# Attention kernel: softmax tiles as the stationary operand of the value products, and outputs reshaped through memory

## What is computed

```python
def _masked_attention(xf, Wq, Wk, Wv, lookahead):
    q = jnp.einsum('bnd,hed->bhne', xf, Wq)
    k = jnp.einsum('bnd,hed->bhne', xf, Wk)
    v = jnp.einsum('bnd,hed->bhne', xf, Wv)
    s = jnp.einsum('bhqe,bhke->bhqk', q, k) * scale
    mask = i[:, None] <= i[None, :] if lookahead else i[:, None] >= i[None, :]
    s = jnp.where(mask, s, jnp.finfo(s.dtype).min)
    p = jax.nn.softmax(s, axis=-1)
    return jnp.einsum('bhqk,bhke->bhqe', p, v)
...
o = jnp.concatenate([o_lb, o_la], axis=1)   # (B, 16, T*F, 64)
o = o.reshape(B, T * F, D)                  # no transpose: heads stay apart
out = jnp.einsum('bnd,od->bno', o, Wo)
return x + out
```

## Time and profile before

| | us |
|---|---|
| median of 3 runs | 3389.85 (3389.22 to 3391.37) |
| the profiled execution | 3386.05, span 3384.2 |
| TensorE busy | 3179.4 (94%), 14472 products |
| TensorE weight loads | 2443.1 (72%) |
| VectorE busy | 2062.4 (61%) |
| ScalarE busy | 1740.3 (51%) |
| GpSimd busy | 1672.8 (49%) |
| mean granted clock of TensorE | 0.986 |

### The profile page before, as it was taken

How to read it: one execution, slowest core, us unless ns; L and a number is a source line. 1 busy time by engine, 2 the same in 40 slices (tenths; PEclk the granted TensorE clock), 3 DMA queues, 4 the chain that set the end, 5 groups by cost and what they waited for, 6 DMA issues and landing times.

```text
span 3384.2 us, 50386 instructions
## 1 busy us (share of the span) xinstructions
PE 3179.4 (94%) x14472; PEld 2443.1 (72%) x14472; DVE 2062.4 (61%) x3452; ACT 1740.3 (51%) x3525; POOL 1672.8 (49%) x1306
## 2 busy tenths in 40 slices
PE   4999998999999679999999999999999999999998
PEld 3888887788888457766777767777777677767776
DVE  6212111410110488888888888888888887888885
ACT  2100110210100267777767777777777777777775
POOL 2000000100000367777777777777777777777774
PEclk9999999999999789999999999999999999999999
DMA  6325223422311232111212111212121112111210
GB/s 236 100 84 135 95 66 82 154 71 50 97 62 49 64 84 60 59 54 44 56 50 69 44 56 50 69 44 57 51 69 44 51 56 69 44 50 57 62 39 19
DMA packets 142547, 232.93 MB, mean 69 GB/s; under 512 B 76800, under 2 KB 76800, under 8 KB 142336
## 3 DMA queue, kind: packets, MB, share of 16 engines
q1 hardware_dynamic: 142336, 230.73, 22.9%
HBM read 163.58 MB, written 67.11 MB: 68 GB/s over the span
## 4 chain that ended last, share of the span: by engine, by line
PE 28%; POOL 13%; DVE 11%; issue 9%; DMA 1%; ACT 1%; POOLq 0%; DVEq 0%; SPq 0%; ACTq 0%
POOL p_low L691 6%; POOL k L716 4%; PE acc L1058 4%; PE acc L1062 4%; PE max L1014 4%; PE acc L1060 4%; PE scores L1044 4%; PE scores L1039 3%; DVE o_full L983 3%; PE rows L1076 3%; DVE part_max L929 2%; POOL q L712 2%; DVE p_low L691 2%; PE side L1024 1%; DVE diagonal L702 1%
## 5 line engine op out<-in xcount | busy, mean ns | idle before, releaser
L691 POOL TENSOR_TENSOR p_low<-probs,p_high 128x512 fp32r<-128x512 f32 (+2 forms) x960 | 1191.3, 1257 | 575.0 <-ACT p_high L864 539.3
L860 ACT ACTIVATE probs<-scores 128x512 f32<-128x512 f32 (+3 forms) x1280 | 684.1, 534 | 411.0 <-PE scores L1044 390.5
L929 DVE TENSOR_REDUCE part_max<-max 128x1 f32<-128x512 f32 (+3 forms) x1280 | 766.1, 603 | 197.8 <-PE max L1014 178.2
L864 ACT ACTIVATE p_high<-scores 128x512 fp32r<-128x512 f32 (+3 forms) x1280 | 683.3, 534 | 0.0
L1014 PE MATMUL max<-k,q 128*128 128x512 f32 (+3 forms) x1280 | 490.1, 384 | 75.3 <-DVE part_max L929 37.4
L1044 PE MATMUL scores<-q,k 128*128 128x512 f32 (+3 forms) x1280 | 506.2, 395 | 0.0
L1058 PE MATMUL acc<-p_high,v 128*128 128x512 f32 (+3 forms) x1280 | 479.8, 375 | 27.4 <-POOL p_low L691 19.4
L318 DVE COPY stage_d<-proj 128x512 f32<-128x512 f32 x96 | 66.0, 689 | 707.8 <-PE proj L264 459.5
L1039 PE MATMUL scores<-q,k 128*128 128x512 f32 (+3 forms) x1280 | 478.5, 374 | 10.5 <-ACT p_high L864 7.5
L1062 PE MATMUL acc<-p_low,v 128*128 128x512 f32 (+3 forms) x1280 | 469.0, 366 | 0.0
L1060 PE MATMUL acc<-p_high,v 128*65 128x512 f32 (+3 forms) x1280 | 462.4, 361 | 0.0
(11 more groups left out here) (94 smaller groups left out, 5027.8 us busy)
## 6 DMA issues: line engine op xcount, KB each, us to landing
raw<-qk_s SPq DMA_DIRECT2D x256, 256.0 KB, 4.2
xs<-xT SPq DMA_DIRECT2D x64, 512.0 KB, 4.9
w_raw<-wqk SPq DMA_DIRECT2D x32, 512.0 KB, 3.7
qk_s<-stage_a SPq DMA_DIRECT2D x64, 256.0 KB, 2.4
qk_s<-stage_d SPq DMA_DIRECT2D x64, 256.0 KB, 2.4
raw<-v_s SPq DMA_DIRECT2D x64, 256.0 KB, 2.8
res<-x_res SPq DMA_DIRECT2D x32, 512.0 KB, 4.4
out<-res SPq DMA_DIRECT2D x32, 512.0 KB, 2.6
```

Of the source, the lines that this page charges most:

```text
L691: eng.tensor_tensor(p_low[:, n % 4, part], probs[:, n % 4, part], p_high[:, n % 4, part].bitcast(F32), ALU.subtract).then_inc(done, 1)
L860: nc.scalar.activation(probs[:, n % 4, 0:cols], scores[n % 2][:, 0:cols], ACT.Exp, scale=SCALE).then_inc(exp_done, 1)
L864: nc.scalar.activation(p_high[:, n % 4, 0:cols], scores[n % 2][:, 0:cols], ACT.Exp, scale=SCALE).then_inc(high_act, 1)
L929: nc.vector.tensor_reduce(part_max[:, s % 2, at, m:m + 1], max_bank[n % 2][:, 0:cols], AX.X, ALU.max).then_inc(max_read, 1)
```

## The change

Value products: for each block of 128 queries of a tile, p_high is loaded as weights and v streams past it with 130 columns (64 high, a one, a zero, 64 low), then p_low with 66 (high, one, zero). The sums now stand with queries on the partitions, two blocks to a bank: `acc_early` (one bank) for the two blocks of a stage that are complete first, `acc_late` (two) for the others. ScalarE copies them out in two halves (early, late); VectorE takes the reciprocal of the column of ones, adds the two halves of the sums and multiplies, 256 elements a partition each.

The reshape: each quarter of a head's o is stored to `o_s` in memory (store) and the whole is loaded back as 128 rows of 1024 (back). TensorE turns it in eight transposes through the bank `side` (turn, slots 10 and 14); ScalarE and VectorE take o_high and o_low from that bank (round, rest). The projection uses `side` too, and the bank `rows` is gone. Its six pieces move to slots 21, 22, 23, 30, 31, 32.

The row of maxima is made by four products of minus_max, broadcast as weights, with a unit matrix. The masks of the scores are fp32r. SP's transfers are issued by slot numbers too.

```diff
-DIAGONAL_SLOT = {2: 4, 3: 17, 0: 22, 1: 30}
-SHIFT_SLOT = {2: 6, 3: 19, 0: 24, 1: 32}
+SHIFT_SLOT = {2: 5, 3: 18, 0: 27, 1: 35}
...
-OP_SLOT = {0: 9, 1: 10, 2: 11, 3: 15, 4: 16, 5: 17}
-ADD_SLOT = {0: 13, 1: 19}
+BACK_SLOT = 5
+TURN_SLOT = {0: 10, 1: 14}
+OP_SLOT = {0: 21, 1: 22, 2: 23, 3: 30, 4: 31, 5: 32}
+ADD_SLOT = {0: 25, 1: 34}
...
 # shift
-                    nc.tensor.matmul(side[:, :], v[:, 0, 0, E:E + 1].broadcast_to([P, P]), diagonal[:, :, :],
-                                     start=True, stop=True).then_inc(row_ready, 1)
+                    for r in range(4):
+                        last = nc.tensor.matmul(side[:, r * P:(r + 1) * P],
+                                                minus_max[:, n % 2, r:r + 1].broadcast_to([P, P]), eye_r[:, :],
+                                                start=True, stop=True)
+                    last.then_inc(row_ready, 1)
...
 # turn
+                    pe.wait_ge(o_back, 16 * count(i, p, 1, 0))
...
+                    for r in range(4):
+                        j = 4 * n + r
+                        last = nc.tensor.transpose(side[:, r * P:(r + 1) * P], o_rows[:, j * P:(j + 1) * P], eye[:, :])
+                    last.then_inc(turned, 1)
...
 # values
-                    nc.tensor.matmul(sums[:, col:col + cols], v[:, p, j, 0:P], high, start=first, stop=False,
-                                     skip_group_check=True)
-                    nc.tensor.matmul(sums[0:E + 1, col:col + cols], v[:, p, j, P:VC], high, start=False,
-                                     stop=False, skip_group_check=True)
-                    nc.tensor.matmul(sums[:, col:col + cols], v[:, p, j, 0:P], low, start=False, stop=final,
-                                     skip_group_check=True).then_inc(weighed, 1)
+                    for r in blocks if kind == LB else reversed(blocks):
+                        order = r if kind == LB else 3 - r
+                        first, early = at == 0 and order % 2 == 0, order < 2
+                        if first and early:
+
+                            reached(pe, early_copied, count(i, p, STAGES, s))
+                        elif first:
+
+                            reached(pe, late_copied, count(i, p, STAGES, s - 1))
+                        bank = acc_early if early else acc_late[s % 2]
+                        to, part = r % 2 * VC, slice(r * P - col, (r + 1) * P - col)
+                        nc.tensor.matmul(bank[:, to:to + VC], p_high[:, n % 4, part], v[:, p, j, :],
+                                         start=first, stop=False, skip_group_check=True)
+                        final = order % 2 == 1 and at == 4 * s + order
+                        last = nc.tensor.matmul(bank[:, to:to + LOW_V], p_low[:, n % 4, part], v[:, p, j, 0:LOW_V],
+                                                start=False, stop=final, skip_group_check=True)
+                    last.then_inc(weighed, 1)
...
 # SP
+                elif step == "store":
+                    sp.wait_ge(o_ready, done)
+                    sp.dma_start(dst, o_n[:, n % 2, :, :]).then_inc(o_stored[n % 2], 16)
+                elif step == "back":
+                    for half in range(2):
+                        sp.wait_ge(o_stored[half], 16 * count(i, p, 2, 0))
...
+                    sp.dma_start(o_rows[:, :], o_s[bass.ds(head - 1, 1)].rearrange("a (r q) e -> (a r) (q e)", q=16)
+                                 ).then_inc(o_back, 16)
```

## The result

The kernel after takes 4118.06 us (median of 4 runs, 4108.85 to 4139.79) against 3389.53 us for the kernel before in the same job. The ratio is 1.216 (95% interval 1.213 to 1.219). I had forecast 3680 us with a range from 3540 to 3800. The sign was right, and the size was less than half of what came: +729 us instead of +292.

The account below looks back on a forecast made before the run. Slots 0 to 20 were bound by a chain through GpSimd and transfers, the rest by TensorE; 36.5 + 39.9 us made a head 76.4 against 67.34, +281 over 31 heads, +4 first, +7 end: 3680 us, range 3540 to 3800.

Parts of the forecast that it names:

- Value products at 0.11 us: Full tile: eight products, each priced at its weight load's 0.11 us, 0.88 against 0.70, +0.18 us per full tile.
- Rivals B and C: Value products: B, loads hide, 3395 us (0.04; half way 3560, 0.05); C, loads fetched further ahead, faster (0.04).
- Second part, 39.9 us: Slots 21 to 39: 25.59 us grows to 39.9, of it 11.2 for the 48 projection products that nothing covers there.
- The clock: TensorE's work in both parts: products priced at the profile's steps, such as 0.2325 us a projection product.
- rival D: Slot 10: TensorE stands some 4 us for o, granted clock falls; up to 3.5 us more a head, 3790 us, chance 0.14.
- The chain that gives way in the first part: Slots 0 to 20: eighth split at 34.56 us, then GpSimd straight on to tile 20; 36.5 us in place of 41.75.
- GpSimd's wait of 2.38 us: Behind the eighth split: GpSimd waits for TensorE, busy with projection products; after the change GpSimd goes straight on.
- The granted 4 us of room for transposes and waits: First part: TensorE has 4 us to spare, covering transposes (0.9 to 3.2 us) and early-bank waits at slots 4 and 12.
- GpSimd's stretch: GpSimd's p_low averages 1386 ns, 1.29 us when quiet; 1.3 us (0 to 1.7) of the chain's stretch given back.
- The shift on TensorE and fp32r masks as nothing: Shift row: +0.21 us each, two in each part of the head; masks within +-0.1 us per head, taken as nothing.

Follow-up runs that it names:

- b2_late_projection: Kernel before with only the projection pieces moved to slots 21, 22, 23, 30, 31, 32 and the adds to 25, 34; 3771.51 us, ratio 1.113.
- a5_wide: Kernel after with every value product streaming 256 columns, same count of products and weight loads; 3856.74 us, ratio 1.138.
- a3_early_return: Kernel after, loading rows of q and k long in memory in place of o, at slot 0 without waiting for the stores; 4137.72 us, ratio 1.223.
- b8_thin_ahead: Kernel before without 36 of 48 projection products a head, next head's maxima 21 units ahead instead of 23; 3359.78 us, ratio 0.991.
- b6_thin_projection: Kernel before with 36 of the 48 projection products a head left out, all else unchanged; 3375.14 us, ratio 0.996.
- a6_wide_ahead: Kernel after with 256-column value products and the next head's maxima 21 units ahead instead of 23; 3796.84 us, ratio 1.120.
- b3_shift_pe: Kernel before with only the row of maxima made by four products instead of VectorE's diagonal; 3394.54 us, ratio 1.002.
- b1_streams: Stand-alone streams of products on constant tiles, attention left out; thin pairs took 0.213 us a product, products of 130 columns 0.111.

## Why the forecast failed

In the order of its sum, in mean heads (forecast 77.3, measured 92.4, miss 15.1):

- **Value products at 0.11 us: right**, at full clock: 1.59 us a full slot against 1.58. The same product costs 0.21 at half clock. Rivals B and C, in which weight loads hide, are refuted by that: single steps differ (0.07 and 0.15 us in the lines from 3347.00 on), but their mean stays at the load's 0.11. The Trainium skill's 81 ns for loads and products of 128 columns (TensorE: Matmul & The Clock Gate, Back-to-back issue gap) did not appear either; the gapless stream of 130 columns took 111.
- **Second part, 39.9 us: right.** 40.8 measured, of it 4.6 at half clock, and 39.7 where the clock is kept, 1.0 of it (13 tiles at 0.08) for the wider products. The projection out of cover costs what it weighs. b2_late_projection alone shows +9.9.
- **The clock: wrong, the largest step.** My sum prices all work at full clock and has no term for losing it. I looked for a danger only in rival D, put it down to TensorE standing for o, and gave the kernel up to 3.5 us a head for it. Measured: a5_wide's head less what its columns cost (28 full tiles x 0.08 = 2.2; the cut tiles, some 0.5 more, are left out) is 81.6, so the clock that a5_wide wins back is worth an estimated 10.8 us a head, some 335 us in all. It still has 4.7 us at half clock, worth at most 2.4 more. And the cause is not the return of o (a3_early_return) but what comes after a wait: with thin products the half clock lasts 16.0 us a time, with wide ones 3.8.
- **The chain that gives way in the first part: wrong, 5.5 us.** In a5_wide the first part is 44.1, less 1.2 for its columns 42.9, where I had 37.4. The eighth split ends 2.0 us later than in my sum (37.1 against 35.1), some of which is the wider columns and the clock again. The rest is behind it: I let GpSimd go "straight on" to p_low of tile 20 and the values follow in 0.88 us, 2.24 us in all. Measured are 7.0 us in a5_wide, and 5.7 even in b8_thin_ahead, with a quarter of the projection and the wait moved. I also put GpSimd's wait of 2.38 us there down to the projection and so let it go. But the way from the eighth split to tile 20 takes 7.2 us in the kernel before and 7.4 in b6_thin_projection, which has 36 of the 48 products less. The step that failed is that I followed one engine's list and not TensorE's: the max product at slot 17 waits for the eighth split, and the scores of tile 20, the values of slots 17, 18 and 19 and three more slots' products stand behind it in order. So the projection in slots 9 to 17 was nearly free. b6_thin_projection puts a bound on it: without 8.4 us of it the mean head is no shorter, and with all of the clock lost there added they are worth some 3 us. That this order accounts for all of the 5.5 us is argued; what the runs show is 2.0 us of it, by moving the product (a6_wide_ahead).
- **The granted 4 us of room for transposes and waits: half right.** Over the 29 heads of the kernel after the wait of the transposes for o is 1.2 us a head. The wait for the early bank is 0.3, 0.9 and 1.0 us a head at slots 0, 4 and 12, of which I had said for 4 and 12 that it falls under the chain; at slot 24, where I had put 0.8, TensorE does not wait. Both waits lie in the first part, and stretches at half clock begin at them. The head shown above loses its clock at 3296.00, right behind such a wait:

```profile
3295.91 0.32 PE L1133 MATMUL acc_early<-v,p_high 128*128 128x130 f32 x1 [1.13 <-ACT acc_s L933]
```

- **GpSimd's stretch** went the way I said: p_low of 512 columns fell from 1386 ns to 1286. It did not show in the time.
- **The shift on TensorE and fp32r masks as nothing: right for the shift** (b3_shift_pe, +0.2%). The masks were not tried alone.

Together: 77.3 + 10.8 (clock) + 5.5 (chain) - 1.2 (second part) is 92.4. The parts are differences of the same means, so that they add up says nothing by itself. The chance I gave the case in which TensorE's clock falls was 0.14, and I priced it at up to 3.5 us a head, with the load of k in it, where the clock alone is worth 10.8. The earlier trace rows had the sign of it: a stretch with the clock at 0.75 while TensorE was busy 62.86 of 85 us. I read it as "broken work", when the question was what TensorE streams after a wait.

What stays open: a5_wide's remaining 4.7 us at half clock and the 11.3 in b2_late_projection, which has no thin value products, begin at waits of TensorE (in a5_wide at slots 0, 1, 10, 12 and 17, in b2_late_projection at 2 to 4, 13, 14 and 17). Taking one wait away took the loss at its slot away (slot 17 in a6_wide_ahead), but the half clock of the head did not fall with it (5.4 against 4.7 us), and no run took them all. Of the 2.0 us at the eighth split, o's return is no part that a3_early_return could show; what of it is the order of the other work is not shown.

## What to carry to other kernels

Price work on TensorE at the clock it will have, not the one in the profile: before replacing wide products with thin ones, ask whether the new mix is ever interrupted, since after an interruption it may have to win the full clock back, and products bound by their weight loads did not in the streams and took 16.0 us on the mean in the kernel. Work that lies beside a chain through other engines gives nothing back when it leaves, and costs its full weight where it goes; to see what such a chain is, follow the in-order list of every engine behind the event, the busy one first. Taking the work out without putting it anywhere (b6_thin_projection) is a cheap test and would have told it.

A version faster than the kernel before came out of the search: b7_ahead, at 0.997 (0.996 to 0.998), by putting the product that waits for the last split of k one slot further back.

## What the runs showed of the hardware

- Thin pairs (130 and 66 columns, each with a weight load of 128) that keep TensorE busy for 110 of 110 us ran at a granted clock of 0.50, products of 130 columns entered at full clock at 1.00: 0.213 against 0.111 us a product. Entered at half clock, these too stayed at 0.50. The Trainium skill (TensorE: Matmul & The Clock Gate, Part 1: The HAM clock gate) says that TensorE is throttled unless activity releases it. If activity is read as the profile's busy time, these runs disagree, and the measurement decides: TensorE was busy for all of the 110 us, and the clock did not come back.
- The clock has a memory. One and the same slot ran at 1.58 us and full clock for 63 us when entered at full clock, and at 2.98 us and half clock for 119 us when entered at half clock, and also after a pause of 11 us. Slots of 512-column products came back to full clock from either, and stayed there.
- The kernels lost the clock at waits: all 208 stretches at half clock, in 29 heads each of four kernels, begin in a wait of TensorE of 1 us or more or within 2.3 us behind one. Not every wait does it: a5_wide has 120 waits of 1 us or more and 36 such stretches, and b1_streams kept the clock through 39 waits of 0.7 us between products of 512 columns. In the stream of thin pairs it fell without a wait, 5 us after the stream's start.
- More columns per product made the kernel 261 us faster (a5_wide against after), at the same count of products.
